# A graph layer with gathers on GpSimd: pacing the gathers by VectorE's operations

## What is computed

```
h = maximum(layernorm(x), 0)
e_feat = concatenate([h[src], h[dst], edge_attr])            # 96 numbers per edge
v = relu(e_feat @ W1 + b1) @ W2 + b2                         # 64 hidden, 32 out
out = x + maximum(segment_max(v, dst), h)
```

## Time and profile before

| | us |
|---|---|
| median of 3 runs | 4759.94 (4747.39 to 4760.97) |
| the profiled execution, its own time | 4765.93 |
| its span, first to last instruction | 4764.1 |
| granted TensorE clock, mean over the span | 0.801 of full speed |

### The profile page before, as it was taken

The page is one execution under the profiler, slowest core; times in us unless marked ns, Lnnn a source line. Parts: engine busy times, 40 slices in busy tenths (PEclk is TensorE's granted clock), DMA queues, the critical chain, the costliest instruction groups (busy, mean ns, idle before and its releaser), DMA issues.

```text
span 4764.1 us, 41821 instructions
## 1 busy us (share of the span) xinstructions
PE 2960.5 (62%) x11492; PEld 2111.3 (44%) x11492; DVE 2078.8 (44%) x3562; ACT 748.1 (16%) x1058; POOL 2733.4 (57%) x2852
## 2 busy tenths in 40 slices
PE   1266566567676666666666666565766656565677
PEld 0144344445454444444444444444544444444445
DVE  5044344444444444444444444343444434444447
ACT  3011111111111111111111111111111111111111
POOL 6456555556665556565566556555655555565550
PEclk8578778788787878887888887778878888787788
DMA  4322222222222222222222222222222222221222
GB/s 99 76 58 53 46 54 47 52 49 59 49 53 47 56 50 55 50 54 47 53 51 51 54 49 51 51 47 52 55 48 50 47 53 51 49 58 43 53 52 44
DMA packets 245595, 252.33 MB, mean 53 GB/s; under 512 B 83265, under 2 KB 199479, under 8 KB 239113
## 3 DMA queue, kind: packets, MB, share of 16 engines
q10 hardware_dynamic: 20790, 103.55, 9.1%
q1 hardware_dynamic: 133938, 101.54, 7.4%
q0 software_dynamic: 90784, 46.48, 7.1%
HBM read 239.86 MB, written 11.52 MB: 53 GB/s over the span
## 4 chain that ended last, share of the span: by engine, by line
another core or an unknown queue 44%; PE 21%; DVE 15%; issue 14%; DVEq 3%; ACT 3%; ACTq 1%; SPq 0%; DMA 0%; POOL 0%; POOLq 0%
PE ps_spare L570 11%; DVE sel_tmp L958 3%; DVE running L929 3%; DVE best L995 3%; PE ps_turned L603 2%; DVE key_hot L947 2%; DVEq L989 2%; PE ps_hid L582 2%; PE ps_val L591 1%; PE ps_feat L537 1%; PE ps_hid L580 1%; DVE edge_hot L940 1%; PE ps_picked L612 1%; DVE feat L965 1%
## 5 line engine op out<-in xcount | busy, mean ns | idle before, releaser
L480 POOL DMA_INDIRECT feat<-h_rows,idx x2821 | 2716.6, 963 | 1900.3 <-issue 993.3
L570 PE MATMUL ps_spare<-table,key_hot 128*128 128x448 f32 x5642 | 1500.6, 426 | 395.6 <-DVE sel_tmp L958 348.0
L570 PEld LDWEIGHTS ps_spare<-table,key_hot 128*128 128x128 f32 x5642 | 1259.8, 230 | 524.3 <-DVE sel_tmp L958 339.0
L958 DVE SCALAR_TENSOR_TENSOR sel_tmp<-off_place,offset,ps_spare 128x448 f32<-128x448 f32 x403 | 273.6, 679 | 1553.4 <-remote 1234.1
L603 PE MATMUL ps_turned<-ident,running 128*128 128x128 f32 x806 | 171.9, 351 | 939.4 <-DVE running L929 733.7
L722 ACT ACTIVATE hidden<-ps_hid,b_col 128x1024 f32<-128x1024 f32 x202 | 224.8, 1113 | 2681.5 <-remote 2196.6
L603 PEld LDWEIGHTS ps_turned<-ident,running 128*128 128x128 f32 x806 | 116.2, 175 | 1088.5 <-DVE running L929 805.1
L980 DVE TENSOR_TENSOR ends<-ps_turned,ends 128x512 fp32r<-128x512 f32 x202 | 139.5, 690 | 786.4 <-ACT ends L734 579.8
L995 DVE TENSOR_TENSOR best<-ps_picked,best 32x64 f32 x1612 | 355.0, 220 | 162.9 <-remote 96.6
L947 DVE TENSOR_TENSOR key_hot<-dst_rows,ps_iota 128x1792 fp32r<-128x1792 f32 x202 | 406.1, 2011 | 18.1 <-DMA dst_rows<-key_rows 18.1
L580 PE MATMUL ps_hid<-feat_t,w_blk 128*128 128x512 f32 x806 | 413.8, 595 | 0.0
(11 more groups left out here) (125 smaller groups left out, 893.7 us busy)
## 6 DMA issues: line engine op xcount, KB each, us to landing
dst_rows<-loc_rows ACTq DMA_DIRECT2D x98, 512.0 KB
feat_t<-attr_rows_in ACTq DMA_DIRECT2D x98, 512.0 KB
feat<-h_rows,idx POOLq DMA_INDIRECT x2821
dst_rows<-key_rows SPq DMA_DIRECT2D x101, 256.0 KB
term_ring<-term_rows SPq DMA_DIRECT2D x404, 64.0 KB
dst_rows<-keep_rows SPq DMA_DIRECT2D x100, 256.0 KB
term_rows<-best SPq DMA_DIRECT2D x3, 1792.0 KB
idx<-src_cols_in SPq DMA_DIRECT2D x51, 32.0 KB
```

Source lines behind the costliest of these rows:

```text
L480: nc.gpsimd.indirect_dma_start(feat[:, slot, k, :], None, h_dram, bass.IndirectOffsetOnAxis(ap=idx[:, c % IDX, k:k + 1].bitcast(U32), axis=0),
L570: mm = pe.matmul(ps_sel, key_hot[:, c // TWO % 2, g, P * (c % TWO):P * (c % TWO) + P], table[half][:, g, :], start=(g == 0 and half == 0), ...
L958: nc.vector.scalar_tensor_tensor(out=sel_tmp[:].rearrange("p (f a) -> p f a", a=SA), in0=off_place[:].unsqueeze(1).broadcast_to([P, D, SA] ...
```

## The change

Only GpSimd's list changes. A new function `follow` stands in front of gathers 0, 3, 6, 9 and 11 of a pair's 14: GpSimd waits there for one of VectorE's operations of the step two pairs back (`LEAD` = 2). The old wait for the slot stays.

```
+LEAD = 2
...
+            def follow(i, v, n):
+
+                if n == 0 and (not known(i) or v >= 2):
+                    pool.wait_ge(S["run_ready"], i * UNROLL + v - 1)
+                elif n == 3:
+                    pool.wait_ge(S["edge_hot_ready"], i * UNROLL + v + 1)
+                elif n == 6:
+                    pool.wait_ge(S["sel_ready"], i * IDX + TWO * v + 3)
+                elif n == 9:
+                    pool.wait_ge(S["hots_made"], i * UNROLL + v + 3)
+                elif n == 11:
+                    pool.wait_ge(S["sel_ready"], i * IDX + TWO * v + 4)
+                else:
+                    return
+                pool.sem_inc(S["followed"], 1)
...
                 for k in range(GK):
+                    if c >= TWO * LEAD or not known(i):
+                        follow(i, c // TWO - LEAD, c % TWO * GK + k)
                     nc.gpsimd.indirect_dma_start(
```

More of the change, by code:

```diff
@@ L186, in gnn_layer @@
             base_step fall_done keep_staged end_staged half_ready end_turned end_kept loc_staged stage_pad zeros_ready term_stored
-            chunk_begun feat_turned feat_t_ready edge_hot_ready hid_sum hid_ready val_sum val_ready
+            chunk_begun followed feat_turned feat_t_ready edge_hot_ready hid_sum hid_ready val_sum val_ready
             best_half run_ready ends_turned ends_ready ends_split pick_ready best_done best_zero
```

## The result

The changed kernel takes 4618.03 us (4614.99 to 4620.15), the kernel before beside it 4753.66 us (4707.94 to 4760.97): a ratio of 0.9734, with a 95% interval from 0.9671 to 0.9797. I had forecast 4848 us, in a range from 4450 to 5130. The change is 2.7% faster where I had it 2% slower. The profiled execution took 4619.54 us, 146.4 us less than that of before.

A forecast was written before the change was run, and what follows sets the result against it. The bound was taken to be a pair's 14 gathers (17.5 us) plus the pause in which they drain. 4765.93 - 95 + 67 + 116 = 4854 us, less 6 for profiled over median, gave 4848, range 4450 to 5130.

The forecast's parts named there:

- 217 + 199 P: Whole kernel: profiled time in us after the change, with P the length of each of 199 steps loaded with gathers.
- P = 23.3: Loaded step in us: 17.5 of gathers plus a 5.3 pause for every 12.75 gathers; 22.70 before.
- Setup, -95 us: Before the first pair: fewer gathers hold TensorE's updates, so the last `node_terms` copy stands at 103.7 instead of 198.66 us.
- The waits themselves, 0: GpSimd's list: five added waits and increments per pair cost nothing, apart from a 0.75 us start after idleness.
- The last steps, +67 us: End of the pairs: six steps that ran free of gathers at 12.19 us become loaded steps, 11.1 us more each.
- A step in the loop, +0.6 us: The 193 loaded steps: each goes from 22.70 to 23.3 us, 116 us in all.
- some 6 us: Within a run of gathers: by this time into it TensorE's updates are late again.
- works in part: Rival, loaded steps: runs of 14 or more survive with short 4.0 us pauses; P = 21.5, 4490 us, chance 0.20.
- not moved: Rival, loaded steps: P stays 22.7, only setup and last steps show; 4728 us, chance 0.10.
- Two stops a step: Rival, loaded steps: first selection late, then transposed ends late in a new run; P = 25, 5186 us, chance 0.13.
- the pacing breaks the bursts: Rival, loaded steps: short pauses keep TensorE's updates prompt, near GpSimd's own 17.5 us; P = 18.5, 3893 us, chance 0.10.
- The gathers beside VectorE: Pairs' stretch: by the skill's rule, gathers placed beside other VectorE operations would win 30 us at most, 0.6%.

The follow-up runs named there:

- e1: Changed kernel with its waits only in front of gathers of pairs 8 and later: 4682.8 us, 0.987 of the kernel before on the same chip.
- e4: Changed kernel with only the wait in front of gather 0 (for the scan) left: 4805.4 us, 1.013 of the kernel before on the same chip.
- e3: Changed kernel with only the wait in front of gather 11 (second selection's picking) left: 4624.2 us, 0.975 of the kernel before on the same chip.
- e5: Changed kernel with only gather 11's wait left, for the second picking's product instead of its sum: 3704.7 us, 1.014 of the kernel before on chip 10.
- e10: Changed kernel with only gather 11's wait left, for the second picking's product, run on chip 5: 3705.0 us, 1.015 of the kernel before there.
- e13: Changed kernel with a one-column memset and a wait for it ahead of every third gather, on chip 11: 4324.6 us, 1.183 of the kernel before there.
- e18: Changed kernel with a one-column memset and a wait for it ahead of every third gather, on chip 4: 4329.7 us, 1.185 of the kernel before there.

## Why the prediction was wrong

**The sum.** The form, 217 + 199 P, was right: with the measured 22.17 it gives 217 + 4412 - 6 = 4623 us, 5 from the result. What failed is one term, P = 23.3.

**Setup, -95 us:** right, 99.2. The drain after 31 gathers was 2.4 us, not 4.7, and the copies came 1.6 us apart, not 2.1. That gathers had held them is shown by e1, where the waits stand later and `node_terms` is late again.

**The waits themselves, 0:** right. The gathers stay 0.30 us apart across the four waits that are met in time, and a start after idleness took 0.79 us.

**The last steps, +67 us:** 54, the same error in P and one step of 16.1 us.

**A step in the loop, +0.6 us:** wrong, -0.52, and this is the step of the prediction that failed. I wrote that gathers close up into one run and that the pause after it is drain, VectorE and start; that is so. I then listed three places at which VectorE could stop, with 9, 11 or 11 to 14 gathers let go, and took a mean over them: 5.3 us for every 12.75. In the changed kernel there is no such mixture. It stands at one place, the second selection, with 14 gathers behind every stop, and the pause that I had worked out for a selection, 4.85 us, is what it costs: 4.77, counted from the end of a gather, or 4.5 beyond the usual 0.30. With 17.5 + 4.85 = 22.35 the same sum would have given 217 + 199 x 22.35 - 6 = 4659. Why this place: the run is begun by VectorE's second picking, so TensorE's next handoffs lie at fixed times in it. The ends, the features and the first selection (6.4 us) come promptly, the second selection (11.5 us) does not. I had counted how many gathers are let go before each stop, and not when in the run the update falls for which VectorE would stop. Following one period would have put the first selection at 6.4 us. It would not have settled that it is prompt there. By the trace of before it need not be: of the selections that TensorE ended 6.0 to 6.5 us into a run, all of them the second of a step, 14 of 16 were late, which my "some 6 us" agrees with. In the changed kernel none of 67 first selections in the same half microsecond was late. So the time since the run began is not the whole condition, and what else decides is open. Nor do updates come only with the drain, as I wrote: the selection taken at 2487.01 came through 2.5 us before the last gather of its burst had ended.

**The rivals.** The result lies between "works in part" (4490) and "not moved" (4728). The former, to which I gave 0.20, has the mechanism right: runs of 14 survive, each pause is of the short kind, and the detour of 8.12 us by scan and transposes is gone. Its step of 17.5 + 4.0 us was 0.7 short of the measured 22.17, most of it the pause, 4.5 us beyond the cadence. That the measured time lies in my wide range is no merit of the forecast, which had the direction wrong. "Two stops a step" (5186) did not occur. The first wait alone (e4) shows how near the slow side was: a run that begins behind the scan already loses 1.3% against before. A run that begins earlier than after the second picking was measured on no holding chip. The five groups as such gain nothing (e3), and my rival "the pacing breaks the bursts" had no run of three gathers to stand on.

**The ground beneath it.** I took the late updates for a property of the kernel. e5 to e10 and e13 to e18 show that it goes with the chip: the kernel before takes 3650 to 3654 us on five of the seven numbered chips. There the change costs 1.6%. Nothing in one trace of before could tell me that. Each chip was visited once, so a state of the chip that passes is not ruled out.

**The gathers beside VectorE.** The mean gather takes 960 ns in the pairs' stretch, as before. By the rule of the Trainium skill, SBUF — State Buffer, "SBUF: two separate sides", gathers that are placed otherwise beside VectorE might have won up to 30 us; the trace shows none of it.

## What to carry to other kernels

Where an engine's work is released in runs by another's progress, look for one period that repeats, and price that before a mean over the places where it might stop: here the mean gave 23.3 us and the one place 22.35, where 22.17 was measured. Choose with care the operation that releases a run: on the same holding chip a wait for the picking alone gains 2.5% (e3), and one for the scan behind it alone loses 1.3% (e4). Whether an earlier release gains more was not measured where it matters. Before tuning against a delay that the profile calls remote, measure the kernel on several chips, since what pays on one kind costs on the other.

## What I had not expected of the hardware

Chips differ in whether TensorE's updates are held beside GpSimd's gathers, and by 30% in this kernel's time (4740 to 4754 against 3650 to 3654 us). In the changed kernel an update that TensorE makes up to 7.5 us into a run of gathers comes promptly (4 late in 306 between 5 and 7.5 us). Between 7.5 and 10 us it depends: the second layers that end there are prompt, about half of the picked columns are not. Beyond 10 us, 193 of 194 second selections and all 194 first layers were late. These times are not a rule for all kernels on a holding chip: in the trace of before, 41 of 84 selections between 5 and 7.5 us were late. On the other chips no update was late beside 2790 gathers in a row. After a run's last gather the first late update is taken 2.6 us later for runs of 14 and 4.7 for runs of 28 (medians over the traces of the holding chips). After the three runs of 112 in the setup it was 3.9 to 4.5 us, and in the trace of before updates went on being late until 194.4, 14.4 us after the run. So the wait for the first update does not simply grow with the run. The cause is open.

One more thing goes with it. The traces of the changed kernel on a holding chip and on chip 5, their lines on the gathers in the list of DMA issues (engine, operation, count, median us from issue to landing):

```profile
feat<-h_rows,idx POOLq DMA_INDIRECT x2821
```

```profile
feat<-h_rows,idx POOLq DMA_INDIRECT x2821, 3.3
```

The landing time is missing on the holding chip because most landings are not in its trace: of the 2821 x 16 = 45,136 increments that the gathers make, it holds 11,348, and the trace of chip 5 holds 44,745. All traces of holding chips are like the one (13,407 to 16,883 landings of all DMAs), those of the others like the second (51,641 to 51,979 with fourteen gathers). So the chips also differ in how many semaphore events their traces hold. The gaps follow the run: in the holding trace of the changed kernel 11.4 landings are on record in the fifth microsecond of a run of 14 and at most 3.2 in any from the eleventh to the twentieth (means over 180 runs). The Trainium skill, NOTIFIC — the notification-queue block, "7.1 Overflow: three behaviours, one of which stalls the engine", says that a full record queue drops records, new or old, or stalls its producer, depending on how it was set, and its section 10 reports no overflow at 6.6 million records a second, a rate that was not a ceiling. From the cadence, 16 increments every 1.25 us make 12.8 million a second, an estimate above that rate. By that rule the hold could be the recording of semaphore events and not the kernel's own traffic. Two things speak against taking that as settled. The holding traces miss records, which is the dropping and not the stalling, and no run shows that anything stalled besides. And the trace of chip 5 holds 57,642 semaphore updates in 3709.8 us, 15.5 million a second, with none late. No run here had fewer events at the same gathers, none was taken on a holding chip with the gathers spaced, and whether the times would differ without recording no run shows, so this is a possibility and no finding.
